# First mixing in 32-row form between the dense second convolution and the second mixing, with the banks used in turn

## The reference, cut to what matters

```python
def mixed(x, cond, W0, b0, W1, b1, W2, b2, weight, bias_k):      # layers 0 and 2
    h = gelu(cond @ W0 + b0); h = gelu(h @ W1 + b1)
    att = softmax(h @ W2 + b2)                                   # 8 weights for each image
    return einsum('boi,bih->boh', einsum('bk,koi->boi', att, weight[..., 0]), x) + (att @ bias_k)[:, :, None]

def conv(x, c, weight, c_weight, bias):                          # layers 1 and 3: 9 taps, 4 groups of 32 channels
    return conv1d(x, weight, pad=4, groups=4) + (c @ c_weight.T)[:, :, None] + bias[None, :, None]

x = x + mixed(x, ...0); x = x + conv(x, ...1); x = x + mixed(x, ...2); x = x + conv(x, ...3)
```

## Time and profile before

| what | value |
|---|---|
| median of three runs | 2648.64 us (2647.57 to 2649.98) |
| the profiled execution's own time | 2650.44 us |
| its span | 2648.6 us |
| busy: TensorE matmul | 2627.4 us, 99% |
| busy: TensorE weight load | 1808.4 us, 68% |
| busy: VectorE | 2143.3 us, 81% |
| busy: ScalarE | 2034.7 us, 77% |
| busy: GpSimd | 818.0 us, 31% |
| granted TensorE clock | 0.999 |
| time of packets on SP's DMA queue | 58.7% of 16 engines' span |

### The profile page before, as it was taken

The page is one execution under the profiler, slowest core; times in us unless marked ns, Lnnn a source line. Parts: engine busy times, 40 slices in busy tenths (PEclk is TensorE's granted clock), DMA queues, the critical chain, the costliest instruction groups (busy, mean ns, idle before and its releaser), DMA issues.

```text
span 2648.6 us, 106673 instructions
## 1 busy us (share of the span) xinstructions
PE 2627.4 (99%) x42610; PEld 1808.4 (68%) x42610; DVE 2143.3 (81%) x3093; ACT 2034.7 (77%) x3605; POOL 818.0 (31%) x1040
## 2 busy tenths in 40 slices
PE   9999999999999999999999999999999999999997
PEld 6667666766676667666766676667666766676665
DVE  8888788878887888788878887888788878887884
ACT  7777777777777777777777777777777777777774
POOL 1233233323332333233323332333233323332332
PEclk9999999999999999999999999999999999999999
DMA  4565556555655565556555655565556555655554
GB/s 166 182 205 185 180 184 195 187 180 184 196 187 180 184 195 187 180 183 196 187 180 183 194 189 180 183 195 188 180 183 195 188 180 183 195 189 180 182 176 149
DMA packets 228046, 489.82 MB, mean 185 GB/s; under 512 B 47016, under 2 KB 129072, under 8 KB 195376
## 3 DMA queue, kind: packets, MB, share of 16 engines
q1 hardware_dynamic: 228016, 489.39, 58.7%
HBM read 205.04 MB, written 150.99 MB: 134 GB/s over the span
## 4 chain that ended last, share of the span: by engine, by line
PE 98%; DVE 1%; ACT 0%; issue 0%; DVEq 0%; ACTq 0%
PE ps L361 42%; PE ps L342 28%; PE ps L313 14%; PE ps L326 13%; DVE y L680 0%; DVE y L674 0%; DVE xp L652 0%; DVE m_sum L632 0%; DVE prod L627 0%; PE ps L259 0%; DVE y_full L703 0%; PE ps L428 0%; PE ps L301 0%; PE ps L264 0%; DVE x_t L715 0%
## 5 line engine op out<-in xcount | busy, mean ns | idle before, releaser
L361 PE MATMUL ps<-y,conv_parts 32*128 32x512 f32 x18432 | 1141.7, 395 | 3.9 <-DVE y_full L703 1.8
L361 PEld LDWEIGHTS ps<-y,conv_parts 32*128 32x128 f32 x18432 | 906.5, 183 | 283.1 <-issue 131.4
L781 POOL COPY bias<-bias_table 128x4 f32 (+3 forms) x512 | 317.6, 621 | 1795.5 <-DMA o_ch<-o_ph 896.9
L680 DVE TENSOR_TENSOR y<-y_full,y 128x512 fp32r<-128x512 f32 x1020 | 636.6, 688 | 221.9 <-ACT y L497 221.9
L342 PE MATMUL ps<-y_full,conv_raw 32*32 32x512 f32 (+1 forms) x16384 | 753.8, 596 | 1.7 <-DVE y_full L703 1.7
L491 ACT ACTIVATE y_full<-ps,bias 128x512 f32<-128x512 f32 x1016 | 602.6, 707 | 26.6 <-issue 16.2
L546 ACT ACTIVATE o_ph<-ps,bias 128x512 f32<-128x512 f32 x508 | 308.5, 693 | 371.5 <-PE ps L361 371.5
L497 ACT CAST y<-y_full 128x512 fp32r<-128x512 f32 x1020 | 566.8, 663 | 0.7 <-DVE y_full L703 0.7
L342 PEld LDWEIGHTS ps<-y_full,conv_raw 32*32 32x32 f32 (+1 forms) x16384 | 275.5, 116 | 408.4 <-issue 406.2
L787 POOL COPY o_t<-o_ch 128x512 f32<-128x512 f32 x508 | 528.5, 1186 | 26.9 <-DMA o_ch<-o_ph 26.9
L491 ACT ACTIVATE y<-ps,bias 128x512 fp32r<-128x512 f32 x516 | 313.0, 690 | 191.3 <-PE ps L342 176.6
(11 more groups left out here) (60 smaller groups left out, 74.6 us busy)
## 6 DMA issues: line engine op xcount, KB each, us to landing
x_t<-x SPq DMA_DIRECT2D x128, 1024.0 KB, 5.0
o_ch<-o_ph SPq DMA_DIRECT2D x2032, 64.0 KB, 2.0
out<-o_t SPq DMA_DIRECT2D x127, 1024.0 KB, 4.0
m_parts<-mixed SPq DMA_DIRECT2D x512, 128.0 KB, 2.6
mixed<-m_own SPq DMA_DIRECT2D x128, 128.0 KB, 1.7
conv_raw<-conv_w SPq DMA_DIRECT2D x2, 768.0 KB, 9.8
mix_sb<-mix_w SPq DMA_DIRECT2D x2, 576.0 KB, 7.4
out<-x_t SPq DMA_DIRECT2D x4, 256.0 KB, 4.2
```

The costliest lines, as they stand in the source:

```text
L361: ins = nc.tensor.matmul(ps[:, bank + t, :], conv_parts[layer][rows, w, s - DENSE[0], :], src[rows, a, p_in, q:q + N], start=first, stop=f ...
L680: nc.vector.tensor_tensor(dst, full, high.bitcast(fp32), ALU.subtract).then_inc(low_set[layer], 1)
L781: nc.gpsimd.tensor_copy(bias[layer][:], bias_table[:, bass.ds(j, 1), COLUMN[layer]:COLUMN[layer] + WIDTH[layer]].rearrange("c j g -> c (j ...
```

## The change

In steps of the loop the first mixing is issued as 48 matmuls of 32 rows and stands between the dense part of the second convolution and the second mixing. It writes banks 4 to 7 (image 3 on), and the second mixing banks 0 to 3 (but for the first and the last image). The matrix of the first mixing (image 3 on) is made one step earlier, stored to memory and loaded back in 32-row groups, as that of the second, and x is loaded in four pieces, so that a partition group holds the channels' rows for one place range. VectorE reads the fourth bank of the output (`output_last`) and of the first mixing (`full_0_last`); ScalarE reads three of each, and its reading of the first mixing moves into the step before. VectorE's list and SP's list get a new order. The core of the diff:

```diff
 TensorE
-            def second_mix(j):
+            def first_mix(j):
 
-                pe.wait_ge(m_in, 16 * G * (j + 1))
+                pe.wait_ge(m_in[0], 16 * G * (j - WHOLE + 1))
+                pe.wait_ge(low_set[1], 4 * (j - 1))
+                for g in range(G):
+                    pe.wait_ge(x_low_set, nth(j - 1, g))
+                    for n, (m, a) in enumerate(PASSES):
+                        first, final = g == 0 and n == 0, g == G - 1 and n == len(PASSES) - 1
+                        for q in range(G):
+                            rows = slice(CG * q, CG * (q + 1))
+                            ins = nc.tensor.matmul(ps[:, first_bank(j) + q, :], m_parts[0][rows, g, m, :], xp[rows, a, g, :],
+                                                   start=first, stop=final)
+                            if final:
+                                ins.then_inc(mm[0], 1)
...
+                            if first:
+                                wait_bank(p)
+                            ins = nc.tensor.matmul(ps[:, second_bank(j) + p, :], m_parts[2][rows, g, m, :], y2[rows, a, g, :], start=first, stop=final)
...
+                def free2(p):
+                    if (inner or i > 0) and not (not inner and i == B - 1):
+                        output_read(i - 1, p)
...
+                if has(i, inner, -2) and (inner or i > 0):
+                    first_mix(i + 2)
                 if has(i, inner, 0):
-                    second_mix(i)
-                if has(i, inner, -2):
-                    first_mix(i + 2, free0)
+                    second_mix(i, free2)
 ScalarE
-                if has(i, inner, -1):
-                    full_0(i + 1, 1 - odd)
                 high_2(i - 1, not inner and i == 1)
...
                 output(i - 1, not inner and is_last(i), not inner and i == 1)
+                if has(i, inner, -2):
+                    full_0(i + 2, odd)
                 if has(i, inner, 0):
                     full_2(i, False)
 VectorE
+            def full_0_last(j, odd):
...
+                dve.wait_ge(mm[0], nth(j, q))
+                nc.vector.tensor_scalar(segment(y1_full[odd], q), by_phase(first_bank(j) + q), bias[0][:, 0:1], None, ALU.add).then_inc(full_last, 1)
...
+            def output_last(j, first):
...
+                dve.wait_ge(mm[3], nth(j, g))
+                nc.vector.tensor_scalar(o_ph[:, g, :], ps[:, g, :], bias[3][:, g:g + 1], None, ALU.add).then_inc(phases_last, 1)
...
-                if has(i, inner, -2):
-                    matrix(0, i + 2)
-                    halves(0, i + 2)
                 low_2(i - 1)
                 if has(i, inner, -2):
                     x_low(i + 2)
                 if has(i, inner, 0):
                     low_1(i)
                 if has(i, inner, -1):
+                    low_0(i + 1, 1 - odd)
+                if inner or not is_last(i):
+                    output_last(i - 1, not inner and i == 1)
+                if has(i, inner, -3):
+                    matrix(0, i + 3)
+                if has(i, inner, -2):
+                    full_0_last(i + 2, odd)
+                if has(i, inner, -3):
+                    halves(0, i + 3)
+                if has(i, inner, -1):
                     matrix(2, i + 1)
                     halves(2, i + 1)
-                    low_0(i + 1, 1 - odd)
 SP
-                sp.dma_start(flat(x_t, "q n"), x[j]).then_inc(x_in, 16)
+                for q in range(G):
+                    sp.dma_start(x_t[CG * q:CG * (q + 1)],
+                                 x[j].rearrange("(g c) (q n) -> q c g n", g=G, q=G)[q]).then_inc(x_in, 16)
...
+                for p in range(PH):
+                    if p == 1 and matrix is not None:
+                        sp.wait_ge(stored[2], 16 * matrix + 16)
                     sp.dma_start(o_ch[CG * g:CG * (g + 1), p, :], o_ph[CG * p:CG * (p + 1), g, :]).then_inc(shuffled[p], 16)
...
-                if has(i, inner, -1):
-                    store_matrix(i + 1)
-                if has(i, inner, 1) and (inner or not is_last(i)):
-                    for g in range(G):
-                        shuffle(i - 1, g)
-                if has(i, inner, -1):
-                    load_matrix(i + 1, False)
+                moves = has(i, inner, 1) and (inner or not is_last(i))
+                if moves:
+                    shuffle(i - 1, 0)
+                    shuffle(i - 1, 1)
...
+                if has(i, inner, -3):
+                    store_matrix(0, i + 3)
+                if moves:
+                    shuffle(i - 1, 2)
+                if has(i, inner, -1) and (inner or i > 0):
+                    store_matrix(2, i + 1)
+                if moves:
+                    shuffle(i - 1, 3, i + 1 if inner else None)
+                if has(i, inner, -3):
+                    load_matrix(0, i + 3, False)
+                if has(i, inner, -1) and (inner or i > 0):
+                    load_matrix(2, i + 1, False)
```

More of the change, by code:

```diff
@@ L160, in has, with second_bank, first_bank @@
             return inner or 0 <= i - lag < B
+        def second_bank(j):
+            return 4 if isinstance(j, int) and j in (0, B - 1) else 0
+        def first_bank(j):
+            return 0 if isinstance(j, int) and j < WHOLE else 4
         def nth(j, k):
@@ new lines, in load_matrix @@
+            def load_matrix(layer, j, first):
+                if layer == 0:
+                    sp.wait_ge(mm[0], 4 * j)
+                    sp.wait_ge(stored[0], 16 * j - 16 * (WHOLE - 1))
+                else:
+                    if not first:
+                        sp.wait_ge(mm[2], 4 * j)
+                    if isinstance(j, int):
+                        sp.wait_ge(stored[2], 16 * j + 16)
+                for q in range(G):
+                    sp.dma_start(m_parts[layer][CG * q:CG * (q + 1)].rearrange("c g w o -> c g (w o)").bitcast(fp32),
+                                 scratch[layer // 2][bass.ds(j, 1)].rearrange("s (g c) w o -> (s c) g (w o)", g=G)).then_inc(m_in[layer], 16)
@@ L213, in shuffle @@
+            def shuffle(j, g, matrix=None):
+                if g == G - 1:
+                    sp.wait_ge(phases_last, j + 1)
+                else:
+                    sp.wait_ge(phases_set, 3 * j + g + 1)
                 for p in range(PH):
+                    if p == 1 and matrix is not None:
+                        sp.wait_ge(stored[2], 16 * matrix + 16)
                     sp.dma_start(o_ch[CG * g:CG * (g + 1), p, :], o_ph[CG * p:CG * (p + 1), g, :]).then_inc(shuffled[p], 16)
@@ L492, in from_bank, with high_of_full @@
                                      bias=bias[layer][:, k % WIDTH[layer]:k % WIDTH[layer] + 1]).then_inc(done[layer], 1)
-            def high_of_full(layer, count, full, dst):
-                act.wait_ge(full_set[layer], count)
+            def high_of_full(layer, count, full, dst, last=False):
+                if layer == 0 and last:
+                    act.wait_ge(full_last, count)
+                else:
+                    act.wait_ge(full_set[layer], count)
                 nc.scalar.copy(dst, full).then_inc(high_set[layer], 1)
@@ L502, in full_of_first @@
                     act.wait_ge(low_set[0], q + 1)
[L503 removed]
+                    nc.scalar.activation(segment(y1_full[0], q), by_phase(q), ACT.Identity,
+                                         bias=bias[0][:, 0:1]).then_inc(full_set[0] if q < G - 1 else full_last, 1)
             def full_0(j, odd):
[L507 to L508 removed]
+                for q in range(G - 1):
+                    from_bank(0, j, q, by_phase(first_bank(j) + q), segment(y1_full[odd], q), full_set)
             def high_0(j, odd):
@@ L526, in full_2 @@
                     act.wait_ge(mm[3], 4 * j)
-                for p in range(PH // 2 if isinstance(j, int) and j >= B - 2 else PH):
-                    from_bank(2, j, p, ps[:, 4 + p, :], y3_full[:, p, 1:N + 1], full_set)
+                for p in range(PH // 2 if isinstance(j, int) and j == B - 1 else PH):
+                    from_bank(2, j, p, ps[:, second_bank(j) + p, :], y3_full[:, p, 1:N + 1], full_set)
             def high_2(j, first):
@@ L534, in high_2 @@
                 for p in range(PH):
-                    high_of_full(2, 4 * (j + 1) if isinstance(j, int) and j >= B - 2 else nth(j, p), y3_full[:, p, 1:N + 1], y3[:, HIGH, p, 1:N + 1])
+                    high_of_full(2, 4 * (j + 1) if isinstance(j, int) and j == B - 1 else nth(j, p), y3_full[:, p, 1:N + 1], y3[:, HIGH, p, 1:N + 1])
             def output(j, final, first):
-                for g in range(G // 2 if final else G):
+                for g in range(G // 2 if final else G - 1):
                     act.wait_ge(mm[3], nth(j, g))
@@ L738, in step @@
                     conv_low_part(3)
+                    matrix(0, 3)
+                    full_0_last(2, 0)
+                    halves(0, 3)
                     return
-                if has(i, inner, -2):
-                    matrix(0, i + 2)
-                    halves(0, i + 2)
```

121 lines of the change are left out of this document (73 added, 48 removed).

## The result

The changed kernel takes **2759.9 us** (median of four runs, 2759.17 to 2762.68) against 2649.31 for the kernel before, a ratio of **1.042, 95% interval 1.0402 to 1.0438**: 4.2% slower, where the prediction said 1.9% faster. Its profiled span is 2757.4 us.

A forecast was written before the change was run, and what follows sets the result against it. TensorE, busy throughout the 20.38 us step, was taken as the bound. 2648.6 - 52.5 (125 steps x 0.42) + 2.3 (head) + 0.3 (tail) = 2598.7, said as 2599 us; range 2593 to 2605.

The forecast's parts named there:

- 19.3 of 19.96: SP's list of issues per step: with the new stores, loads and x quarters it takes 19.3 of the 19.96 us step.
- Hidden, by 0.6: SP's list, with the first mixing's matrix going through memory, stays hidden behind TensorE's step with 0.6 us spare.
- 18.9, shorter than the list: Path from shuffles through GpSimd's copies to out: now 16.8 us, 2.1 longer after the change, still below SP's list.
- the turns: Rival, chance 0.28: GpSimd's copies and VectorE's subtractions alternate, VectorE loses 2.35 us, step 20.15, time 2624, up to 2640 us.
- The edges: TensorE's changes between 128-row and 32-row matmuls lose 0.24 and 0.18 us; removing both saves 0.42 per step.
- The rounds of the new first mixing: First mixing on TensorE in 32-row form: 12 rounds of four matmuls at 0.233 us, 2.80 us.
- Head and tail: First and last steps of the run: VectorE's lateness costs some 2.3 us, waiting for output readings near the end 0.3.
- VectorE's two readings and its list: VectorE reads bank four twice, 0.66 us each; its list takes 17.9 of 19.96, with 2.2 to lose per step.
- Edges aren't the cause: Rival, chance 0.06: TensorE's lost time comes with order or semaphores and moves along; 2648 to 2652 us.
- Shut out for all four copies: Rival, chance 0.11: VectorE's subtractions wait until GpSimd's four copies end; step 20.93, time 2718 us.
- The third output reading: Rival, chance 0.06: ScalarE's third reading comes late, 0.16 us spare isn't enough; 0.1 to 0.3 per step, 2611 to 2636 us.
- The reading of the fourth bank: Output's fourth bank: a fourth reading on ScalarE would end at 2.87 and cost 0.42 us per step, so VectorE takes it.

## Why the prediction was wrong, point by point

**The step that failed** is the one on SP's list and the path through GpSimd, "19.3 of 19.96", "Hidden, by 0.6" and "18.9, shorter than the list". Which transfers come and what stands behind the wait were seen; but the path through GpSimd was summed too short, taken as hidden behind the list, and is the one that sets the step. Measured in the changed kernel against the prediction, for the path:

| term | predicted | measured |
|---|---|---|
| first to last shuffle, with stores and wait | 11.6 | 12.47 |
| of it, shuffles stalled behind x and out | 0 | 1.15 |
| of it, wait for the store's landing | 1.1 | 0.79 |
| last shuffle to first copy | 2.65 | 2.91 |
| first copy to next first shuffle | 4.7 | 5.78 |
| of it, fourth copy behind VectorE's product | 0 | 1.0 |
| sum | 18.9 | 21.17 |

- *The stall* came with x and out in flight, as the run with a small out shows. The prediction looked at a mean share (0.59, going to 0.70) and called it enough. The stage's own row said otherwise before the change: 0.95 in the dense part of the second convolution, when x and out move. In the kernel before, SP's next shuffle came 4 us after out at 1317.67, since it stands one step behind the one at 1301.24; the change took that gap away, and the shuffles stalled behind x and out. Mean share 0.79 instead of 0.70.
- *The copies* take 5.1 on the mean and not 4.13. The prediction had the turns as a rival, with copies that end 1.1 later, but put the loss on VectorE and left the path at 18.9. Here GpSimd is the one on the bounding path: the fourth copy and the product L704 meet, and both get longer (the product 1.80 for 1.35, the copy 2.17 for 1.10 in the step shown). The Trainium skill, "SBUF — State Buffer", section "SBUF: two separate sides", calls the shared pair an exclusive lock; the traces agree, with the copy ending 1.0 behind the product.
- *Last shuffle to first copy* is 0.26 longer by the bias copy that waits behind VectorE's subtractions, 0.62 and not 0.36.
- *The list itself* takes 20.5 where it hardly waits for GpSimd (the run with two copies), not 19.3; so the step would have missed 19.96 even with the copies hidden.

**What held.** The edges: 0.42 saved per step, measured 20.38 - 19.97 = 0.41 with the trip taken away. The rounds of the new first mixing, 2.80. Head and tail were a little dearer than forecast: 49.9 us less was the sum, 47.0 less is what the kernel without the trip took against the kernel before beside it (2604.13 and 2651.08). VectorE's two readings and its list: not the bound in any run, though its product and subtractions hold up GpSimd. "Edges aren't the cause" is refuted.

**The rivals.** "Shut out for all four copies", with a chance of 0.11, forecast a slower kernel. That the kernel is slower is no merit of it: the mechanism is another. In the step shown the four subtractions at 1307.29 take 2.49, undisturbed, and the copies start at 1309.76, where the subtractions end; it is GpSimd that waits, not VectorE. "Turns" do happen where the copies meet the subtractions, as in the kernel with the stores moved:

```profile
1302.00 3.41 DVE L764 TENSOR_TENSOR y<-y_full,y 128x512 fp32r<-128x512 f32 x4
```

0.92 lost on VectorE instead of the 2.35 reckoned, within its spare time. "The third output reading" is in time.

**The reading of the fourth bank.** The prediction priced a fourth reading on ScalarE at 0.42 per step for the output; it is 0.20. For the first mixing it is nothing on the kernel with the stores moved: there that part of the change isn't needed.

**What stays open.** That the fourth copy and the bias copy wait for VectorE is read from their places in the traces; no run moved the product or the subtractions out of their way, so what that would give isn't known. A transfer of the matrix from partition to partition without memory, and the trip alone added to the kernel before, were not tried.

## What to carry to other kernels

When a change adds issues to a queue that others wait on, follow the queue round until it closes (what does its first transfer wait for, and who makes that), and sum it with the rows at the places where it will stand then; a slack that is the sum of ten terms is not a slack of 0.6. Read the DMA share stage by stage: a transfer issued into a stage at 0.95 is not issued at its median time. And a store whose data is ready long before it is issued can leave a crowded queue for an engine with idle time, as long as it doesn't compete with the load that someone waits for: the two stores moved gave 153 us, x moved cost 34.

## What the runs showed of the hardware that was not expected

- SP's issues got longer with much in flight: 1.66 and 1.10 us for shuffles that take 0.59, with 2 MB issued in the 4 us before; gone when 0.9 MB of them were left out.
- With the 1 MB of x issued from a second queue at the same time, the first queue's loads landed later: 128 KB in 4.5 instead of 2.9 us.
- Of four row groups of TensorE, one whose load went out 0.3 us late for its bank cost 0.20 a step.
- GpSimd's copies and VectorE's operations with two tiles from SBUF held each other up: the fourth copy took 2.17 instead of 1.10 behind a product, which took 1.80 instead of 1.35; a bias copy of 0.19 took 1.22 in the middle of four subtractions; four subtractions beside copies took 3.41 instead of 2.49.
